# Softplus of a selective scan: ScalarE makes its parts, GpSimd leaves the stage, and z goes through Silu on its way out of PSUM

## What is computed

```python
xp, z = split(einsum('bld,ed->ble', x, W_in))           # 512 channels each
xc = silu(conv_b + causal_conv4(xp, conv_w))
dt, Bm, Cm = split(einsum('ble,fe->blf', xc, W_x))      # 128, 16 and 16 wide
delta = softplus(einsum('blr,er->ble', dt, W_dt) + b_dt)
dA, dBx = exp(delta * A), delta * Bm * xc               # 16 states per channel
h = dA * h + dBx                                        # over the 256 tokens
y = (sum over states of h * Cm + xc * Dp) * silu(z)
out = einsum('ble,de->bld', y, W_out)
```

## Time and profile before

| | value |
|---|---|
| median of three runs | 862.36 us |
| the profiled execution's own time | 861.11 us |
| its span, first to last instruction | 859.4 us |
| mean granted TensorE clock | 0.969 of full speed |
| busy: PE, DVE, ACT, POOL | 90%, 74%, 52%, 42% of the span |

### The profile page before, as it was taken

One profiled execution on the slowest core, in us unless ns is written; L12 is line 12 of the kernel. 1 busy time (PEld: TensorE's weight loads), 2 busy tenths in 40 slices (PEclk: granted clock), 3 DMA queues, 4 the chain that ended last, 5 costly groups with the idle time before them and its releaser, 6 DMA issues. The chain is left out here.

```text
span 859.4 us, 12018 instructions
## 1 busy us (share of the span) xinstructions
PE 769.5 (90%) x4058; PEld 566.6 (66%) x4080; DVE 635.9 (74%) x1051; ACT 447.4 (52%) x950; POOL 361.4 (42%) x195
## 2 busy tenths in 40 slices
PE   6972887788877999999999999998689999999996
PEld 2420332334434588898889889987567888787876
DVE  5799999998998888766774776676567463736366
ACT  3557565667656356645672765466444242415141
POOL 9048999978886885111120111111253131313130
PEclk9996999989999999999999999999889999999998
DMA  8000000000000200100000010000121110202001
GB/s 297 11 1 1 0 1 0 0 1 1 0 1 1 99 1 25 50 25 26 26 26 25 24 49 25 19 20 19 55 92 56 37 57 21 71 18 73 18 0 49
DMA packets 10905, 28.37 MB, mean 33 GB/s; under 512 B 1648, under 2 KB 3184, under 8 KB 10736
## 3 DMA queue, kind: packets, MB, share of 16 engines
q1 hardware_dynamic: 10864, 27.86, 9.7%
HBM read 26.80 MB, written 1.05 MB: 32 GB/s over the span
## 5 line engine op out<-in xcount | busy, mean ns | idle before, releaser
L316 POOL TENSOR_TENSOR m_ring<-m_du,m_b_sb 128x1024 f32<-128x1024 f32 x64 | 152.5, 2402 | 26.3 <-ACT m_b_sb L549 23.8
L731 DVE TENSOR_TENSOR_SCAN m_ring<-ps,m_ring 128x1024 f32<-128x1024 f32 x64 | 145.2, 2280 | 3.5 <-ACT ps L581 3.2
L1001 POOL TENSOR_TENSOR a_wl<-raw,a_wh 128x1024 fp32r<-128x1024 f32 x16 | 39.9, 2496 | 233.3 <-ACT a_wh L1198 233.0
L425 PE MATMUL ps<-m_ring,ident 128*128 128x512 f32 x256 | 128.2, 616 | 0.4 <-DVE m_ring L736 0.4
L1489 POOL TENSOR_TENSOR e_wl<-raw,e_wh 128x512 fp32r<-128x512 f32 (+1 forms) x55 | 57.2, 1046 | 164.7 <-ACT e_wh L1605 89.8
L856 PE MATMUL ps<-e_rms_hi,e_wh 128*128 128x512 f32 x200 | 87.0, 435 | 3.6 <-ACT e_sg L1618 3.6
L581 ACT ACTIVATE ps<-m_delta,m_negA 128x510 f32<-128x510 f32 x128 | 82.6, 682 | 6.8 <-DVE ps L724 3.7
L425 PEld LDWEIGHTS ps<-m_ring,ident 128*128 128x128 f32 x256 | 50.9, 199 | 45.8 <-issue 43.1
L858 PE MATMUL ps<-e_rms_hi,e_wl 128*128 128x512 f32 x200 | 79.8, 399 | 0.0
L857 PE MATMUL ps<-e_rms_lo,e_wh 128*128 128x512 f32 x200 | 79.3, 396 | 0.0
L1618 ACT ACTIVATE e_sg<-ps 128x512 f32<-128x512 f32 x50 | 29.4, 589 | 84.3 <-PE ps L858 84.3
(11 more groups left out here) (210 smaller groups left out, 2148.8 us busy)
## 6 DMA issues: line engine op xcount, KB each, us to landing
raw<-in_expert_w SPq DMA_DIRECT2D x30, 384.0 KB, 3.0
raw<-in_attn_w SPq DMA_DIRECT2D x20, 512.0 KB, 3.3
m_first<-in_xT SPq DMA_DIRECT2D x2, 512.0 KB, 5.1
x<-in_x_tok SPq DMA_DIRECT2D x1, 1024.0 KB, 10.5
out<-hid SPq DMA_DIRECT2D x8, 128.0 KB, 2.0
m_first<-in_w_x SPq DMA_DIRECT2D x1, 512.0 KB, 7.2
m_first<-in_w_in SPq DMA_DIRECT2D x1, 512.0 KB, 8.0
raw<-in_w_out SPq DMA_DIRECT2D x1, 512.0 KB, 8.6
```

What stands on the lines that cost most here:

```text
L316: nc.gpsimd.tensor_tensor(split(slot(n)), du[:, pair_of(ph):pair_of(ph) + 2, halves(ph)], b_sb[:, n % B_BUFS:n % B_BUFS + 1, :].to_broadca ...
L425: nc.tensor.matmul(ps[:, Y_BANK + c, :], ident[:, :], slot(n)[:, c * HALF:(c + 1) * HALF], start=False, stop=False, skip_group_check=True) ...
L731: nc.vector.tensor_tensor_scan(slot(n), dA_of(n), slot(n), 0.0, ALU.mult, ALU.add).then_inc(scan_done, 1)
L1001: nc.gpsimd.tensor_tensor(w[1][:, j, :], raw[:, j, :], w[0][:, j, :].bitcast(F32), ALU.subtract).then_inc(w_done, 1)
```

## The change

- Softplus: ACT makes |v| (`abs_v`) and max(v, 0) (`relu_v`) straight from PSUM, e with scale -1, and l = log(e + 1) from e with a bias of 1, so `log_u` no longer waits for DVE's u. DVE makes u and t as before, takes t from max(v, 0) (`relu_rest`) and adds l (`sum_delta`). POOL's four subtractions are gone.
- B and C: the three casts go to ACT (`cast_bc`), the two differences stay on DVE (`rest_bc`).
- PSUM: the delta and z pairs go round a ring of four bank pairs, `2 * (r % 4)`.
- z: Silu on its way out of PSUM, all four chunks, between two table loads ahead of the scan. `silu_z` and `z_ready` go.
- The memset of the decays comes behind all four `du`, and POOL's unit 0 waits for all four.
- `dp_diag` is made after the convolution.

```diff
+    def pair_banks(r):
+        return banks(ps, 2 * (r % 2 if r < DELTA0 else r % 4), 2)
...
-        for c in range(EC):
-            pool.wait_ge(l_ready, c + 1)
-            pool.wait_ge(t_ready, c + 1)
-            nc.gpsimd.tensor_tensor(spl[:, c % 2, :], spl[:, c % 2, :], spt[:, c % 2, :],
-                                    ALU.subtract).then_inc(lt_ready, 1)
...
             if n == 0:
-                pool.wait_ge(du_ready, 2)
-            if n == 2:
-                pool.wait_ge(delta_ready, EC)
-            if n == NS:
                 pool.wait_ge(du_ready, EC)
...
-            if r >= 2:
+            if r >= Z0:
+                pe.wait_ge(pair_free, r - 3)
+            elif r == DELTA0 + 3:
+                pe.wait_ge(bc_rest, 1)
+            elif 2 <= r < DELTA0 + 2:
                 pe.wait_ge(pair_free, r - 1)
...
-                    mm = nc.tensor.matmul(ps[:, 2 * (r % 2) + th, :], lhs, rhs[:, th * HALF:(th + 1) * HALF],
-                                          start=(k == 0), stop=(k == len(steps) - 1))
+                    mm = nc.tensor.matmul(pair_banks(r)[:, th * HALF:(th + 1) * HALF], lhs,
+                                          rhs[:, th * HALF:(th + 1) * HALF], start=(k == 0), stop=(k == len(steps) - 1))
...
-        pe.wait_ge(bc_step, 5)
+        pe.wait_ge(bc_part, 3)
         pe.wait_ge(sel_ready, 3)
-        pe.wait_ge(pair_free, Z0 + EC - 1)
+        pe.wait_ge(pair_free, Z0 + 1)
...
-            nc.scalar.activation(z[:, c, :], banks(ps, 2 * (c % 2), 2), ACT.Copy).then_inc(pair_free, 1)
+            nc.scalar.activation(z[:, c, :], pair_banks(Z0 + c), ACT.Silu).then_inc(pair_free, 1)
...
-        def take_v(c):
+        def relu_v(c):
+            nc.scalar.activation(conv[:, c, :], pair_banks(DELTA0 + c), ACT.Relu, bias=b_dt[c]
+                                 ).then_inc(pair_free, 1)
+        def abs_v(c):
             act.wait_ge(pair_ready, DELTA0 + c + 1)
-            nc.scalar.activation(conv[:, c, :], banks(ps, 2 * ((DELTA0 + c) % 2), 2), ACT.Identity,
-                                 bias=b_dt[c]).then_inc(pair_free, 1)
+            if c >= 2:
+                act.wait_ge(l_ready, c - 1)
+                act.wait_ge(t_ready, c - 1)
+            nc.scalar.activation(spa[:, c % 2, :], pair_banks(DELTA0 + c), ACT.Abs, bias=b_dt[c]
+                                 ).then_inc(abs_ready, 1)
         def exp_v(c):
             act.wait_ge(abs_ready, c + 1)
-            nc.scalar.activation(spa[:, c % 2, :], spa[:, c % 2, :], ACT.Exp).then_inc(e_ready, 1)
+            nc.scalar.activation(spa[:, c % 2, :], spa[:, c % 2, :], ACT.Exp, scale=-1.0).then_inc(e_ready, 1)
         def log_u(c):
-            act.wait_ge(u_ready, c + 1)
+            act.wait_ge(e_ready, c + 1)
             if c >= 2:
                 act.wait_ge(delta_ready, c - 1)
-            nc.scalar.activation(spl[:, c % 2, :], spu[:, c % 2, :], ACT.Ln).then_inc(l_ready, 1)
+            nc.scalar.activation(spl[:, c % 2, :], spa[:, c % 2, :], ACT.Ln, bias=1.0).then_inc(l_ready, 1)
...
-        take_v(0)
-        take_v(1)
+        def cast_bc(k):
+            act.wait_ge(bc_ready if k == 0 else bc_rest, max(k, 1))
+            rows, src = slice(P // 2 if k == 1 else 3 * P // 4 if k else 0, P), banks(ps, 6, 2) if k == 0 else bcr
+            nc.scalar.activation(bcp[rows, :], src[rows, :], ACT.Copy).then_inc(bc_part, 1)
+        cast_bc(0)
+        abs_v(0)
+        relu_v(0)
         exp_v(0)
-        take_v(2)
+        abs_v(1)
+        cast_bc(1)
+        log_u(0)
+        relu_v(1)
         exp_v(1)
-        log_u(0)
-        take_v(3)
+        cast_bc(2)
+        abs_v(2)
+        log_u(1)
+        relu_v(2)
         exp_v(2)
-        log_u(1)
+        abs_v(3)
+        log_u(2)
+        relu_v(3)
+        exp_v(3)
+        log_u(3)
+        nc.scalar.preload_act_table_set("silu_and_others")
         take_z(0)
-        exp_v(3)
-        log_u(2)
         take_z(1)
-        log_u(3)
+        copy_b(0)
         take_z(2)
         take_z(3)
-        copy_b(0)
+        nc.scalar.preload_act_table_set("natural_log_exp_and_others")
         copy_b(1)
         def decay(n):
             ph, s = phase(n), n % NS
             if n >= 2:
                 act.wait_ge(scan_done, n - 1)
+            if n in (0, NS):
+                act.wait_ge(delta_ready, pair_of(ph) + 2)
...
-        act.wait_ge(delta_ready, EC)
         act.wait_ge(a_ready, 1)
         act.wait_ge(dA_zeroed, 1)
-        def silu_z(half):
-            toks = slice(half * HALF, (half + 1) * HALF)
-            act.wait_ge(pair_free, 3 * EC)
-            nc.scalar.activation(z[:, :, toks], z[:, :, toks], ACT.Silu).then_inc(z_ready, 1)
-            nc.scalar.preload_act_table_set("natural_log_exp_and_others")
...
-            if n % (2 * NS) == 1:
-                silu_z(phase(n) // 2)
...
-            nc.vector.tensor_scalar(dp_diag[:, c, :], ident[:], d_p[c], None, ALU.mult).then_inc(dp_ready, 1)
...
-        bc = banks(ps, 6, 2)
-        dve.wait_ge(bc_ready, 1)
-        nc.vector.tensor_copy(bcp, bc).then_inc(bc_step, 1)
...
-            nc.vector.scalar_tensor_tensor(out=spa[:, c % 2, :], in0=conv[:, c, :], scalar=-1.0,
-                                           in1=conv[:, c, :], op0=ALU.mult, op1=ALU.min).then_inc(abs_ready, 1)
+        for c in range(EC):
+            nc.vector.tensor_scalar(dp_diag[:, c, :], ident[:], d_p[c], None, ALU.mult).then_inc(dp_ready, 1)
+        def rest_bc(k):
+            dve.wait_ge(bc_part, k)
+            rows, src = slice(k * P // 4 + P // 4, P), banks(ps, 6, 2) if k == 1 else bcr
+            nc.vector.tensor_tensor(bcr[rows, :], src[rows, :], bcp[rows, :], ALU.subtract).then_inc(bc_rest, 1)
         def one_plus(c):
             dve.wait_ge(e_ready, c + 1)
             if c >= 2:
                 dve.wait_ge(t_ready, c - 1)
-                dve.wait_ge(l_ready, c - 1)
...
             dve.wait_ge(u_ready, c + 1)
             if c >= 2:
-                dve.wait_ge(lt_ready, c - 1)
+                dve.wait_ge(rt_ready, c - 1)
...
+        def relu_rest(c):
+            dve.wait_ge(pair_free, DELTA0 + c + 1)
+            dve.wait_ge(t_ready, c + 1)
+            nc.vector.tensor_tensor(conv[:, c, :], conv[:, c, :], spt[:, c % 2, :], ALU.subtract).then_inc(rt_ready, 1)
         def sum_delta(c):
-            dve.wait_ge(lt_ready, c + 1)
-            nc.vector.scalar_tensor_tensor(out=delta[:, c, :], in0=conv[:, c, :], scalar=0.0, in1=spl[:, c % 2, :],
-                                           op0=ALU.max, op1=ALU.add).then_inc(delta_ready, 1)
+            dve.wait_ge(l_ready, c + 1)
+            dve.wait_ge(rt_ready, c + 1)
+            nc.vector.tensor_tensor(delta[:, c, :], conv[:, c, :], spl[:, c % 2, :], ALU.add).then_inc(delta_ready, 1)
         def times_x(c):
+            if c == 0:
+                dve.wait_ge(bc_part, 3)
             dve.wait_ge(delta_ready, c + 1)
             nc.vector.tensor_tensor(du[:, c, :], delta[:, c, :], xc[:, c, :], ALU.mult).then_inc(du_ready, 1)
-        neg_abs(0)
-        neg_abs(1)
+        rest_bc(1)
         one_plus(0)
-        neg_abs(2)
+        relu_rest(0)
+        rest_bc(2)
         one_plus(1)
-        neg_abs(3)
         sum_delta(0)
+        relu_rest(1)
         one_plus(2)
         sum_delta(1)
+        relu_rest(2)
+        times_x(0)
         one_plus(3)
         sum_delta(2)
-        times_x(0)
+        relu_rest(3)
         times_x(1)
+        times_x(2)
         sum_delta(3)
-        dve.wait_ge(delta_ready, EC)
-        dve.wait_ge(dt_sb_ready, 1)
+        times_x(3)
         decays = ps[:, DA_BANK:DA_BANK + 4, :].rearrange("p k (b t) -> p (k b) t", b=2)
+        dve.wait_ge(pair_free, 3 * EC)
         nc.vector.memset(decays[:, :, 0:1], 0.0).then_inc(dA_zeroed, 1)
-        times_x(2)
-        times_x(3)
...
-            dve.wait_ge(z_ready, ph // 2 + 1)
```

More of the change, by code:

```diff
@@ L186, in mamba_block @@
     dt_ready, dt_sb_ready = sem("m_dt_ready"), sem("m_dt_sb_ready")
-    bc_ready, bc_step = sem("m_bc_ready"), sem("m_bc_step")
-    v_ready, abs_ready, e_ready = sem("m_v_ready"), sem("m_abs_ready"), sem("m_e_ready")
+    bc_ready, bc_part, bc_rest = sem("m_bc_ready"), sem("m_bc_part"), sem("m_bc_rest")
+    abs_ready, e_ready = sem("m_abs_ready"), sem("m_e_ready")
     u_ready, l_ready, t_ready = sem("m_u_ready"), sem("m_l_ready"), sem("m_t_ready")
-    lt_ready, delta_ready, du_ready = sem("m_lt_ready"), sem("m_delta_ready"), sem("m_du_ready")
+    rt_ready, delta_ready, du_ready = sem("m_rt_ready"), sem("m_delta_ready"), sem("m_du_ready")
     a_exp, a_ready = sem("m_a_exp"), sem("m_a_ready")
@@ L193, in mamba_block @@
     ld_xt = sem("m_ld_xt")
-    z_ready = sem("m_z_ready")
     b_ready, b_sb_ready, c_ready = sem("m_b_ready"), sem("m_b_sb_ready"), sem("m_c_ready")
@@ L660, in vector @@
                                                op0=ALU.mult, op1=ALU.add).then_inc(conv_step, 1)
-        bc = banks(ps, 6, 2)
-        dve.wait_ge(bc_ready, 1)
```

(32 more changed lines are left out.)

## The result

The changed kernel takes 854.0 us (852.5 to 854.35, four runs) beside 862.54 us for the kernel before. The ratio is 0.989, with a 95% interval of 0.9875 to 0.9904: 8.5 us faster, where 9.55 were forecast, and inside the stated range. In two later sets the same program came to 854.72 (ratio 0.9912, 0.9897 to 0.9926) and 854.23 us (0.9899, 0.9881 to 0.9916).

A forecast was written before the change was run, and what follows sets the result against it. DVE was taken as the bound before and in the scan, partly held by POOL. Terms -7.9 (scan start) and -1.65 (unit 33) sum to -9.55: 852.8 us against the median, 8 in 10 for 850.3 to 856.2.

The forecast's parts named there:

- DVE is held by POOL, and silence frees it: Softplus: POOL products lengthen DVE's operations; with POOL silent the last `du` ends at 66.6, 11.1 us before 77.69.
- DVE sets the stage from exp 2 on: Softplus: from 52.35 DVE works on to 66.6, with e for chunk 3 there 1.4 us early.
- The loss on the way to unit 4: Scan, units 0 to 4: POOL starts without a lead, losing 0.6 us, so -8.5 becomes -7.9.
- Unit 33: Scan: without Silu of z and its table loads there, DVE's whole wait for the decay goes, -1.65 us.
- `dp_diag`: Ahead of the convolution: moving its four small products leaves the convolution's start unchanged, taken as 0.
- (c): Rival, convolution: it starts at once, 2.2 us more gained, 850.6 us; chance 8%.
- the prediction's "if": Convolution: if `affine_select` holds operations with two SBUF inputs, its start stays, 0; if not, up to 2.2 us earlier.
- The stages behind keep their lengths: Behind the scan: the stages follow in series with unchanged lengths, so the gain ahead reaches the end whole.
- (a): Rival, softplus: Abs and Relu are not in the exp/log table, so loads cost 17.9 us on ACT; 869 us, 3%.
- (b): Rival, scan: POOL paces it, giving back 2 to 4 us; 855 to 857 us, chance 12%.
- (d): Rival, scan: the decay stall at unit 33 moves to another wait, leaving -7.9 alone; 854.5 us, 7%.
- (e): Rival, whole kernel: nothing gained, because the end is set elsewhere; chance 2%.

The follow-up runs named there:

- the late selection: POOL makes the last of the three selections of sel behind the convolution and not ahead of it, against the changed kernel: 854.2 us.

## Why the prediction was right, and where it was off

**DVE is held by POOL, and silence frees it: right.** Taking POOL back in gave +2.5 us from ACT's first read (+3.3 from the span's start) with less work for DVE. The forecast of the last `du`, 66.6, came out at 67.08.

**DVE sets the stage from exp 2 on: right; up to it, ACT does.** The prediction's own times had DVE waiting 0.4 us for exp 1 and 0.5 for exp 2, so by its own numbers ACT paced the stage up to there, but it drew no conclusion from that. Its sum gave ACT 0.92 us a cast. The step behind each cast took 1.08, and the steps ahead of them, from abs 1 and from exp 1, 1.13 and 1.07 where it had 1.00 and 0.95: together 0.57 us. So exp 2 came at 52.9 and not 52.3, and DVE waited 0.57 and 0.89 us. This is, to 0.1 us, what the sum was off by at the last `du` (67.08 for 66.6), at the first scan (69.70 for 69.2) and at unit 4 (81.25 for 80.8). Exp 3 ended at 56.8. ACT's single operations took 1.05 to 1.12 us, but they overlap in steps of 0.95 to 1.0, as the earlier trace rows said; the figures of the Trainium skill ("ScalarE: Activation LUTs", Rules for kernel authors), 0.3 us plus 0.83 ns an element, give an estimate of 1.15 us each and would have put that end near 59.

**The loss on the way to unit 4: right**, 0.56 us for 0.6 (8.02 at the first scan, 7.46 at unit 4), and POOL did catch up. That POOL had been "three units ahead" before is too much: at 3.0 us a unit from 70.13 on the earlier trace rows it had ended two and was in the third at 77.72. The sum didn't use it.

**Unit 33: right in this pair of traces**, 1.72 us from unit 4 to unit 34 (95.25 against 93.53) for 1.65. The number was read from one trace as if the program fixed it. It held in a second trace, but the kernel with Silu put back lost only 0.55 there, and the stretch took 92.73 and 93.77 us in the other two traces of the changed kernel, 95.47 in the other one before. So the nearness of 1.72 to 1.65 is in part luck.

**`dp_diag`: right number, the reason only half right.** The convolution did start before 17 us, at 16.01, which the prediction had named as a sign of (c). But its first product was held (2.63 us), as the prediction's "if" said, and it ended at 32.82, 0.2 earlier than the 33.02 before. "A path that DVE sets", with 2.2 us to be had, is not there. In the trace of the kernel before, PE waited for the last chunk of xc for 0.14 us, at 34 us, and hardly elsewhere; in the changed kernel and in the one with the late selection PE's row of matmuls is unbroken from 7.8 to 37.9 us. So rival (c) could have given some 0.2 us at most even with the hold gone, which a look at PE's timeline would have told.

**"The stages behind keep their lengths": wrong by 0.8 us** in the profiled pair, 562.06 to 562.84. With 9.4 us gained at the statistics this is most of what lies between the forecast and the 8.6 measured. In this pair it is a meeting of DVE and POOL behind attention (below): that step took 4.22 us before and 5.29 after, attention itself 313.8 in both, and the rest 0.3 us less. In the second and third trace of the changed kernel the step took 4.23 and 4.22 us and attention 1.2 us more. The other traces of kernels that touch nothing there lie between 562.4 and 564.2, those of the kernel before both at 562.1. Whether a shift of the start makes the worse cases likelier is open; two or three traces a kernel do not tell.

**The rivals.** (a) is out: no table load among the softplus operations. (b), POOL pacing beyond unit 4, is out: one wait of 0.23 us. (c) is out: the product was held. (d) is out: no wait at unit 34. (e) is out: the gain is clear of the interval.

## What to carry to other kernels

An engine that is idle most of the time can still be the cost: look for operations of one shape with two durations, and ask what ran beside the long one. When one engine is freed, write out the next one's queue with the step of every kind of instruction, casts too, since some 0.3 us a cast was what moved the bound. Count milestones from an event behind the part that varies from trace to trace. And when a wait looks bare, as the 2.56 us ahead of the first scan, price the alternatives: starting POOL sooner lost, giving its first product to DVE and drawing the memset ahead won.

## What was not expected of the hardware

The same two operations, with starts that look alike, held each other in two ways, 1.1 us apart. Behind attention DVE does a chain of small operations beside POOL's split of a weight. DVE and POOL in the changed kernel's first trace:

```profile
604.64 2.17 DVE L845 TENSOR_SCALAR stats<-stats 128x8 f32<-128x8 f32 x1
```

```profile
604.63 1.26 POOL L1488 TENSOR_TENSOR e_wl<-raw,e_wh 128x512 fp32r<-128x512 f32 x1 [0.27 <-ACT e_wh L1597]
605.83 0.95 POOL L1494 MEMSET e_wp<- 128x1024 bf16 x1
```

An operation on 8 columns (0.17 us before) was held for a product and for the memset behind it, to 606.81. In the second trace it began as close (606.48, POOL's product at 606.47), took 0.18 us, and the two-input operation behind it was held instead, for the product alone (1.11 us). The step from attention's last output product to the first row scaled for the experts came to 5.29 us in the one case and 4.23 in the other. The long case stands in ten of the fourteen traces, the short one in four (both of the kernel before, the second and third of the changed kernel). In four of the ten DVE's operation began 0.1 us behind POOL's; in the other ten traces the two recorded starts lie within 0.01 us, six of them long and four short, so the record does not tell what decides. The Trainium skill ("SBUF — State Buffer", Who interferes with whom) says that in a clash whichever issues first has the shared pair of ports for its whole instruction, and that two SBUF inputs compete only with a POOL operation that reads SBUF. The two traces agree with the second point, the memset holding the one-input operation and not the two-input one.

TensorE's clock costs outside PE's own stages too. In the scan, where DVE is the bound, slow sums between 250 and 265 us made DVE wait for a C row 1.70 to 3.33 us in different traces of nearly the same program. In the first two of the changed kernel it was 2.07 us, with a granted clock of 0.50 from 252 to 254, and 2.84, with 0.50 from 250 to 256. With the ring of two it was 3.33, with 0.50 from 254 to 260.
